# A fused attention, graph and transformer kernel: preparation of the output weights done in the second head in place of the first

## The reference

```python
attn = softmax(causal(q @ k.T * scale))
out  = attn @ v
adj  = clip(attn + eye, 0, 1); deg = adj.sum(-1)
feats = v
for l in range(2):
    h = feats @ gnn_w[l] + gnn_b[l]
    feats = gelu((adj @ h) / deg + feats)
out = out + feats @ lin_w + lin_b
y   = layer_norm(concat_heads(out) @ Wo)
```

## Time and profile before

| | |
|---|---|
| median of 3 runs | 1457.83 us |
| lowest and highest | 1454.03, 1460.81 us |
| profiled execution, its own time | 1456.49 us |
| span of its records | 1454.4 us |
| PE busy | 1352.3 us, 93% |
| DVE busy | 1222.5 us, 84% |
| ACT busy | 1002.5 us, 69% |

### The profile page before, as it was taken

One profiled execution on the slowest core, in us unless ns is written; L12 is line 12 of the kernel. 1 busy time (PEld: TensorE's weight loads), 2 busy tenths in 40 slices (PEclk: granted clock), 3 DMA queues, 4 the chain that ended last, 5 costly groups with the idle time before them and its releaser, 6 DMA issues. The chain is left out here.

```text
span 1454.4 us, 27979 instructions
## 1 busy us (share of the span) xinstructions
PE 1352.3 (93%) x9344; PEld 1062.2 (73%) x9344; DVE 1222.5 (84%) x3713; ACT 1002.5 (69%) x2376; POOL 405.8 (28%) x482
## 2 busy tenths in 40 slices
PE   6999999999999999999999999998888999999886
PEld 4678887888888888888788788875555666665663
DVE  6588998899889988999899988976888887887875
ACT  3467776777777777777777777764567778778573
POOL 1022333221321232334324343233223422222211
PEclk9899999999999999999999999999789999999999
DMA  5021111211121121111211123202200101101000
GB/s 141 4 48 38 39 34 42 43 30 34 41 45 30 30 47 42 30 30 40 50 31 30 34 45 72 53 23 65 49 16 20 23 20 23 23 19 23 23 12 22
DMA packets 40666, 53.24 MB, mean 37 GB/s; under 512 B 11679, under 2 KB 23883, under 8 KB 40523
## 3 DMA queue, kind: packets, MB, share of 16 engines
q1 hardware_dynamic: 40522, 51.46, 15.4%
HBM read 9.89 MB, written 1.05 MB: 8 GB/s over the span
## 5 line engine op out<-in xcount | busy, mean ns | idle before, releaser
L1164 ACT ACTIVATE t<-PS 128x512 f32<-128x512 f32 (+3 forms) x384 | 190.1, 495 | 67.8 <-DVE PS L1675 33.1
L1688 DVE TENSOR_TENSOR t<-t 128x512 fp32r<-128x512 f32 (+3 forms) x384 | 211.8, 555 | 7.0 <-ACT t L1165 7.0
L1165 ACT ACTIVATE t<-PS 128x512 fp32r<-128x512 f32 (+3 forms) x384 | 190.2, 495 | 0.0
L1321 ACT ACTIVATE t<-PS,t 128x128 f32<-128x128 f32 x256 | 113.3, 463 | 68.8 <-DVE t L1942 68.8
L745 PE MATMUL PS<-t 128*128 128x512 f32 (+3 forms) x384 | 138.3, 360 | 23.3 <-ACT t L1198 21.6
L1514 POOL TENSOR_TENSOR t<-t 128x16 f32<-128x16 f32 x32 | 92.9, 2902 | 230.8 <-DVE t L1789 230.8
L1478 POOL TENSOR_TENSOR t<-t 128x256 f32<-128x256 f32 x64 | 39.3, 614 | 411.9 <-DVE t L1708 391.0
L664 PE MATMUL PS<-t 128*128 128x512 f32 (+3 forms) x384 | 137.9, 373 | 2.3 <-DVE t L1663 0.9
L694 PE MATMUL PS<-t 128*128 128x512 f32 (+3 forms) x384 | 138.1, 360 | 1.4 <-ACT t L1165 1.1
L1660 DVE CUSTOM_DVE_ANT_0 PS<-PS,t 128x256 f32<-128x256 f32 (+3 forms) x256 | 125.5, 491 | 16.3 <-PE PS L664 15.6
L695 PE MATMUL PS<-t 65*128 65x512 f32 (+3 forms) x384 | 134.6, 351 | 0.0
(11 more groups left out here) (211 smaller groups left out, 3728.4 us busy)
## 6 DMA issues: line engine op xcount, KB each, us to landing
t<-t SPq DMA_DIRECT2D x184, 128.0 KB, 2.2
t<-t SPq DMA_DIRECT2D x62, 256.0 KB, 3.4
t<-in_c_rot SPq DMA_DIRECT2D x4, 512.0 KB, 5.8
t<-in_L_ffn_wqkv SPq DMA_DIRECT2D x2, 768.0 KB, 6.1
t<-in_L_attn_Wv SPq DMA_DIRECT2D x2, 512.0 KB, 7.3
out<-t SPq DMA_DIRECT2D x4, 256.0 KB, 2.3
t<-in_L_ffn_w SPq DMA_DIRECT2D x2, 341.0 KB
t<-in_L_attn_x SPq DMA_DIRECT2D x2, 256.0 KB, 3.2
```

What stands on the lines that cost most here:

```text
L1164: e.activation(Es[:, k % NS, 0:n], b[:, 0:n], ACT.Exp).then_inc(a_es.up((t, k)), 1)
L1165: e.activation(Eh[:, o:o + n], b[:, 0:n], ACT.Exp).then_inc(a_eh.up((t, k)), 1)
L1688: e.tensor_tensor(El[:, o:o + n], Es[:, k % NS, 0:n], f32(Eh[:, o:o + n]), ALU.subtract).then_inc(d_el.up((t, k)), 1)
```

## The change

The whole of `linear` moves from turn 0 to turn 1. On PE, steps 0 to 3 keep their places within the turn, and steps 4 and 5 come earlier in it: behind `smax(t + 1, 5)`, ahead of `scores(t, 7)`. On ACT the copy of step 4 now stands right behind the exponentials of tile 7, ahead of `projv`. On DVE, step 5 stands behind `smax(t + 1, 5)`. The waits follow the banks: `graph1(0, 0)` waits for the values of head 1 in place of `ylin` and `a_lin[4]`, which `projv(2, 0)` now waits for; step 0 waits for `graph1(0, 1)` to be read. No operation is added or taken away.

```diff
--- before.py
+++ after.py
@@ -587,7 +587,7 @@
             def linear(g, b):
                 if g == 0:
                     q.wait_ge(ld["lw"], 16)
-                    q.wait_ge(*d_vb[1, 1])
+                    q.wait_ge(*d_o1[0, 1])
                     m = e.transpose(bank(b)[0:DH, 0:DH], linw[:], identF[0:DH, 0:DH])
                 elif g < 5:
                     q.wait_ge(*d_lin["LB"])
@@ -630,7 +630,8 @@
                 elif t == 0:
                     q.wait_ge(*a_val["W", 1])
                 elif t == 2:
-                    q.wait_ge(*d_o1[0, 1])
+                    q.wait_ge(*a_lin[4])
+                    q.wait_ge(*d_lin["ylin"])
                 else:
                     q.wait_ge(*d_y[t - 3, 1])
                 for k in range(4):
@@ -721,8 +722,7 @@
                 if c:
                     q.wait_ge(*d_o1[t, 0])
                 elif t == 0:
-                    q.wait_ge(*d_lin["ylin"])
-                    q.wait_ge(*a_lin[4])
+                    q.wait_ge(*d_vb[1, 1])
                 elif t % 2 and t + 2 < NH:
                     q.wait_ge(*d_vb[t + 2, 1])
                 else:
@@ -844,26 +844,29 @@
                 smax(t + 1, 1)
                 scores(t, 2)
                 tailT(t - 2, 0)
-                if t == 0:
+                if t == 1:
                     linear(0, 7)
                 scores(t, 3)
                 tailT(t - 2, 1)
                 smax(t + 1, 2)
-                if t == 0:
+                if t == 1:
                     linear(1, 6)
                 av(t, 0)
                 scores(t, 4)
                 smax(t + 1, 3)
-                if t == 0:
+                if t == 1:
                     linear(2, 7)
                 scores(t, 5)
                 tail(t - 2, 0)
                 smax(t + 1, 4)
-                if t == 0:
+                if t == 1:
                     linear(3, 6)
                 scores(t, 6)
                 tail(t - 2, 1)
                 smax(t + 1, 5)
+                if t == 1:
+                    linear(4, 6)
+                    linear(5, 7)
                 scores(t, 7)
                 scores(t, 8)
                 projv(t + 1, 0)
@@ -880,9 +883,6 @@
                 projv(t + 1, 1)
                 av(t, 4)
                 av(t, 5)
-                if t == 0:
-                    linear(4, 6)
-                    linear(5, 7)
                 scores(t, 11)
                 smax(t + 1, 9)
                 av(t, 6)
```

## The result

The changed kernel takes 1462.80 us, median of 19 runs (1459.26 to 1466.92), against 1457.61 for the kernel before in the same runs (1452.99 to 1468.55). The ratio is 1.0034, 95% interval 1.0022 to 1.0045: slower by 3 to 7 us, inside the range predicted and within the 0.5% that I had called no change. The profiled execution took 1460.46 us, span 1458.7.

The account below looks back on a forecast made before the run. PE was taken to set the pace from head 1 on, with room in head 0. From the profiled 1456.49, - 13.1 + 9.65 + 6.5 gave 1459.5 us, read as the same time; range 1450.5 to 1465.5.

Parts of the forecast that it names:

- Term 1: Head 0: without the preparation it gets shorter, -13.1 us, with bounds of -13.8 and about -9.
- The ruler of head 1: Head 1's scores 0 to 8, 9.08 us, taken as measure for head 0 without preparation: 8.6 to 9.1.
- term 2: Head 1: the moved preparation adds +9.65 us: 7.75 work, + 3.65 waits, - 1.75 pauses filled.
- term 3: Head 1: the clock falls to half for 13.6 us, +6.5 us; bounds 0 and about 13.
- the clock holds in head 1: Rival: no low clock in head 1 after the move, sum 1453.0; chance 0.23.
- it comes back soon: Rival: head 1's clock falls but is back within some 4 us, term 3 +2, sum 1455.0; chance 0.12.
- the clock falls in head 0 too: Rival: pauses without the preparation bring a low clock in head 0 as well, 4 us, sum 1463.5; chance 0.10.
- the slower rival: Head 1's clock stays low for a second such stretch, +6.8 us, sum 1466.3; chance 0.06.
- the signs of being wrong: Low clock in head 0, head 1 of 40 us or less, or a difference arising in the transformer block.

Follow-up runs that it names:

- the change's second profile: The changed kernel profiled once more, nothing altered: the long low clock came again in head 1, which took 46.8 us.
- the exchanged kernel: The changed kernel with steps 5 and 4 of the preparation exchanged on PE in head 1: 1456.96 us, ratio 0.9984 to the kernel before.
- The one with the first pause filled: The changed kernel with eight unread matmuls of 128 rows in PE's pause ahead of step 4: ratio 0.9999 to the kernel before.
- half of the change: The changed kernel, but with steps 0 to 3 left in head 0 and only steps 4 and 5 in head 1: 1461.0 us, ratio 1.0017.
- before again: The kernel before profiled once more, nothing altered: head 0 took 38.2 us, with the low clock from 43.7 to 60.7.
- the one on 128 rows: The kernel before with steps 1 to 4 on 128 rows, the added rows zero: ratio 0.9971, head 0 34.01 us.
- both orders mended: The changed kernel with steps 5 and 4 exchanged on PE and ACT's copy of step 4 ahead of tile 7's exponentials: ratio 0.9983, head 1 37.68 us.

## Why the prediction was right

**Term 1, -13.1: measured -13.22.** The ruler of head 1 held: scores 0 to 8 took 9.0 us, up to 49.13, where 8.6 to 9.1 were forecast. Line 731 starts at 55.15, 15.0 us after the first score, where 14.5 to 16 were forecast. That head 0 kept the full clock was in part luck: in the change's second profile it did not.

**Terms 2 and 3, +16.15: measured +16.58.** The order was right: the wait ahead of step 4 (1.91 against 1.85), released by line 1113, the wait ahead of `projv`, then the low clock, and DVE and ACT idle behind PE. The sizes inside the sum were off in opposite ways. Two kernels say how long head 1 of the change would be at full clock. The exchanged one has 39.98 without the first pause; with 1.9 for it, and 0.6 off for its longer DMA wait, that is 41.3. The one with the first pause filled has 42.94, of which the 3.4 us of low clock with PE busy throughout cost half, 1.7, and the DMA wait 0.2 more: 41.0. So term 2 is about +11.2 and not +9.65, and term 3 about +5.4 and not +6.5. These are estimates from one profile each.

- *Term 2* was too small by about 1.5. Its parts: the DMA wait of 0.39 that was put at nothing; three steps at 1.06 because a matmul of another line follows, as 44.70 to 45.76 in the trace before already showed, where I used the 0.96 between two steps, 0.3 together; the wait for `projv`, about 1.6 from the last issue of tile 8 in the exchanged kernel, against 1.3. The rest, 0.5, I have not traced.
- *Term 3* was too large by about 1.1. I took half of 13.6 us as lost, less 0.3. But the second pause, 1.03, lay in the low stretch as a whole. Line 603 lost 2.6 of it (6.25 against 3.66), half of its 5.4 us at the low clock. Without the pause, half would be 6.3; why it came to about 5.4 I have not traced.

**The clock's cause.** The forecast that it would fall in head 1 was right, and so was the long stretch in both profiles; of the reason, only that pauses have a part is supported. I had the low stretch begin "among pauses of PE and steps of 64 rows".

*What starts it.* Steps of 64 rows are not needed: the clock fell ahead of step 1 in three kernels with the preparation in head 0 (43.5, 43.7 and 43.9 us), and at 43.3, 43.5 and 44.6 in head 0 of three profiles with none in it. Filling pauses took the stretch away (head 0 of before) or moved it behind the next pause (head 1 of the change), with every step of 64 rows in its place; exchanging two steps did it without adding anything. But pauses do not bring it each time. In head 0 with the pauses as they are, it fell in 7 of 11 profiles: in all four with steps 0 to 3 there and in three of seven without. With them filled it fell in none of two. So a single profile without a fall is weak evidence, and that the steps have no part in the start is not shown. In head 1, the exchanged kernel has the same pause of 1.42 ahead of `projv` as the one with fillers, and its clock stayed up while the other's fell. Since one kernel can do either in two executions (head 0 of the change), that may need no difference between the two.

*How long it lasts.* In heads 0 and 1 the stretch lasted 13.7 to 17.1 us where steps of 64 rows came in it (before, the change, half of the change), 6.8 with steps 1 to 4 on 128 rows, and 3.4 where none came. The nearest pair is before again, which fell at 43.7 and stayed low for 17.1, and the one on 128 rows, which fell at 43.5 and stayed low for 6.8. That rows decide the length is supported by this one kernel; I have not varied the rows in head 1. Three things limit it. The clock stayed low for 6.5 us after the last such step in the kernel before (53.5 to 60.0) and for 8.2 after line 603 in the change. The second matmul of every score tile has 65 rows, in the short stretches too. And the steps of the preparation are also plain float32, where the matmuls of the scores use the kernel's other form, float32r: a step takes 0.96 us for 512 columns, a matmul of the scores 0.23; the comparisons other than the one on 128 rows can't tell this from the rows.

**The rivals.** That the clock holds in head 1 failed in both profiles of the change. That it comes back soon failed too: it was low for 13.7 us. The Trainium skill, "TensorE: Matmul & The Clock Gate", section "What's actually happening", says that the gate follows how busy PE has been. This case's trace does not agree as long as busy means what the profile draws: PE was busy for 12.77 of 13.80 us at 0.51. That the clock falls in head 0 too, with 0.10, was seen in one of two profiles of the change, and in three of the seven profiles without the preparation in head 0, so 0.10 was low. It costs 1.2 us there, not 4, since it is short. The mechanism of the slower rival, a second low stretch, did not come. A difference did arise in the transformer block, one of the signs of being wrong: 1.5 us of the 4.3, from 2.8 apart where line 944 first runs to 4.3 at the end. It is small, and I have not traced it.

**The whole.** 1459.5 was forecast from the profiled execution, and the changed kernel's own profiled execution took 1460.46. The medians differ by 5.2 us and the sum said 3.0. That the sum came so near is in part luck: terms 2 and 3 were off by 1.5 and 1.1 the opposite ways, and the range of 15 us would have held much more than the mechanism forecast.

## What to carry to other kernels

Moving work out of a stretch with room into one that an engine fills costs about the work even at best: with both orders mended and the clock at full, 7.75 us of PE work cost head 1 7.4, the DMA wait left out. In the change it cost 16.6. Some 3.3 more are two waits for copies by an engine that has other work queued ahead, 0.4 is a wait for a DMA, and about 5.4 the low clock. The room in head 0 was not free either: the preparation cost it 13.2, and 8.2 with the clock kept up. Before moving a step, lay the new order of both engines side by side and look for the wait that a bank or a copy makes: exchanging two independent steps was worth 7 us. And where the trace shows a low clock behind pauses of PE, matmuls that nobody reads, put into the pauses, can cost less than the low clock did; try it, and take more than one profile, as the clock does not fall each time.

## What the runs showed of the hardware

- The same kernel can have a low stretch of the clock in one execution and not in another: head 0 of the change was at 1.00 throughout in one profile, and at 0.50 from 44.6 to 48.1 us in the other. Runs of one kernel differ by 7 us and more (1459.26 to 1466.92 for the change), and such differences may be a part of it.
- In heads 0 and 1, low stretches that hold matmuls of 64 rows were four to five times as long as those that do not (13.7 and 17.1 us against 3.4), while PE was drawn busy in both: 16.80 of 16.80 us, and 3.20 of 3.20. With four of the steps on 128 rows, one such stretch was 6.8 us long.
- Five matmuls without use, 1.2 us of issue, shortened a head by 5 us.
